# Pruning's first row block loaded into the third product's place, with the row blocks taken in another order

## What is computed

```python
att = softmax(Q @ (H.T @ V).T * scale * H, axis=1);  att_scores = att.mean(axis=0)
comp_mask = softmax(0.5 * structural + 0.5 * att_scores) >= th_comp
xn = x_comp / norm(x_comp);  cos = xn @ xn.T
edge_mask = (softmax(cos * H, axis=1) >= th_edge) & comp_mask[:, None]
H_pruned = H * edge_mask
agg = (H_pruned.T * dv_isqrt[None, :]) @ transformed * (1 / H_pruned.sum(axis=0))[:, None]
msg = dv_isqrt[:, None] * (H_pruned @ agg) @ Theta
```

## Time and profile before

| what | us |
|---|---|
| median of 3 runs | 2440.88 |
| lowest, highest | 2438.64, 2444.03 |
| the profiled execution, its own time | 2440.41 |
| its span in the trace | 2438.5 |
| VectorE busy | 1757.7 (72% of the span) |
| TensorE busy | 2055.7 (84%) |
| ScalarE busy | 779.8 (32%) |
| first to last pruning instruction (L1249), both iterations | 712.0 to 1954.2 |

### The profile page before, as it was taken

One profiled execution on the slowest core, in us unless ns is written; L12 is line 12 of the kernel. 1 busy time (PEld: TensorE's weight loads), 2 busy tenths in 40 slices (PEclk: granted clock), 3 DMA queues, 4 the chain that ended last, 5 costly groups with the idle time before them and its releaser, 6 DMA issues. The chain is left out here.

```text
span 2438.5 us, 36215 instructions
## 1 busy us (share of the span) xinstructions
PE 2055.7 (84%) x15608; PEld 732.7 (30%) x15608; DVE 1757.7 (72%) x2037; ACT 779.8 (32%) x990; POOL 4.5 (0%) x18
## 2 busy tenths in 40 slices
PE   6798959989977766699999989987676689996897
PEld 2224324323221111143344323221111134334333
DVE  7875982268879999965541348879999975553998
ACT  0001000146644333311111036653333311111897
POOL 0000000000000000000000000000000000000000
PEclk9999989999988888899999999988888899997999
DMA  9975989989939999987779989929999987763796
GB/s 385 421 336 233 427 356 425 427 328 376 373 132 424 420 411 410 370 317 277 276 278 386 427 326 376 379 106 411 412 411 410 375 330 270 269 252 156 311 421 253
DMA packets 123486, 834.18 MB, mean 342 GB/s; under 512 B 8512, under 2 KB 10560, under 8 KB 76608
## 3 DMA queue, kind: packets, MB, share of 16 engines
q1 hardware_dynamic: 121136, 829.48, 85.0%
q10 hardware_dynamic: 2192, 2.40, 0.3%
HBM read 695.54 MB, written 136.31 MB: 341 GB/s over the span
## 5 line engine op out<-in xcount | busy, mean ns | idle before, releaser
L923 ACT ACTIVATE stream<-stream,negmax 128x4096 f32<-128x4096 f32 x128 | 475.2, 3713 | 521.4 <-DVE negmax L917 521.4
L912 DVE CUSTOM_DVE_ANT_0 stream<-ps,stream 128x1024 f32<-128x1024 f32 x352 | 413.9, 1220 | 55.3 <-PE ps L876 31.9
L876 PE MATMUL ps<-edgeT,node_twice 64*128 64x512 f32 x1024 | 281.0, 669 | 183.5 <-DVE mx L912 183.4
L455 PE MATMUL ps<-stream,stage 128*64 128x512 f32 x1728 | 387.8, 600 | 42.8 <-DMA stream<-in_adjT 27.4
L876 PE MATMUL ps<-edgeT,query_twice 64*128 64x512 f32 x1024 | 249.6, 619 | 6.3 <-DVE edgeT L944 4.0
L1209 PE MATMUL ps<-stream,xw 32*64 32x512 f32 x4096 | 230.5, 595 | 3.7 <-issue 3.0
L455 PEld LDWEIGHTS ps<-stream,stage 128*64 128x64 f32 x1728 | 122.1, 138 | 300.6 <-issue 221.5
L876 PEld LDWEIGHTS ps<-edgeT,node_twice 64*128 64x128 f32 x1024 | 94.2, 201 | 377.9 <-DVE mx L912 267.6
L894 PE MATMUL ps<-stream,ones 128*1 128x512 f32 x1024 | 185.4, 862 | 11.1 <-DVE stream L1249 11.1
L1249 DVE SCALAR_TENSOR_TENSOR stream<-stream,cut 128x4096 f32<-128x4096 f32 x40 | 179.4, 4484 | 1.4
L1427 DVE SCALAR_TENSOR_TENSOR query_twice<-stream,query_twice 128x512 bf16<-128x512 f32 x256 | 154.7, 679 | 4.6 <-ACT query_twice L1405 4.5
(11 more groups left out here) (195 smaller groups left out, 1692.9 us busy)
## 6 DMA issues: line engine op xcount, KB each, us to landing
stream<-in_adj SPq DMA_DIRECT2D x136, 2048.0 KB, 13.0
stream<-in_adjT SPq DMA_DIRECT2D x74, 2048.0 KB, 13.2
pruned<-stream SPq DMA_DIRECT2D x64, 2048.0 KB, 10.5
spare<-in_adj SPq DMA_DIRECT2D x26, 2048.0 KB, 10.3
spare<-pruned SPq DMA_DIRECT2D x22, 2048.0 KB, 11.5
query_twice<-pruned SPq DMA_DIRECT2D x22, 2048.0 KB, 11.3
node_twice<-pruned SPq DMA_DIRECT2D x20, 2048.0 KB, 11.5
query_twice<-in_adj SPq DMA_DIRECT2D x14, 2048.0 KB, 15.7
```

The costliest lines, as they stand in the source:

```text
L455: last = nc.tensor.matmul(ps[F * h:F * h + F, bank + b, :], stage[:, t.k % SL, :], half_bank(src, b, h), start=False, stop=False, skip_gro ...
L876: last = nc.tensor.matmul(ps[:, 2 * slot + h, :], stationary[F * h:F * h + F, rows_n], bank_of(edgeT[F * h:F * h + F, :], c), start=True, ...
L912: nc.vector.tensor_tensor_reduce(out=prod[s][:, cols], in0=ps[:, 2 * slot:2 * slot + 2, :].rearrange("p a b -> p (a b)"), in1=block_in[:, ...
L923: nc.scalar.activation(prod[s], prod[s], ACT.Exp, bias=negmax[:, s:s + 1], accum_out=zsum[:, s:s + 1]).then_inc(exp_done, 1)
```

## The change

Pruning gets a sixth place for a row block, used once: `prod[2]`, the third product, which is first written in step 2. Step 0 takes its row block from there. The order of the blocks and of the places is changed to fit. Steps 1 to 4 take the four blocks left by `attend`, step 5 uses q2. Block 26 is loaded into `prod[2]`, block 27 into q2 right behind it, both at the beginning of the phase. Step 0 frees no place for a load, so that SP issues none after the store of step 0. VectorE waits in step 2 until step 0 is pruned. q2 is last used in step 30 instead of step 29, and chunk 1 is issued a step later.

```diff
-                seq = [*range(22, NB), *range(22)]
-                R, LEAD = 4, 11
+                seq = [26, 22, 23, 25, 24, *range(27, NB), *range(22)]
+                R, LEAD = 5, 11
+                places = [held[0], held[1], held[3], held[2], held[4]]
+                first_loaded = sem("first_block_loaded")
...
                 def buffer(t):
-                    return held[t.k % HELD]
+                    return prod[2] if t.n == 0 else places[(t.n - 1) % HELD]
...
                     def load(n):
-                        sp.dma_start(held[n % HELD], adj_b[seq[n]]).then_inc(loaded[n % HELD], 16)
-
+                        sp.dma_start(places[(n - 1) % HELD], adj_b[seq[n]]).then_inc(loaded[(n - 1) % HELD], 16)
+
+                    sp.dma_start(prod[2], adj_b[seq[0]]).then_inc(first_loaded, 16)
                     load(R)
                     for n in range(NB):
                         sp.wait_ge(pruned, n + 1)
                         sp.dma_start(Hp[seq[n]], prod[n % SL3]).then_inc(stored[n % SL3], 16)
-                        if n + HELD < NB:
+                        if n >= 1 and n + HELD < NB:
                             load(n + HELD)
                         if n == 28:
                             wait_stored(10)
                             load_chunk(0)
-                        if n == 29:
+                        if n == 30:
                             wait_stored(18)
                             load_chunk(1)
...
                     def body(t):
                         s = t.k % SL3
-                        if t.k >= R:
-                            dve.wait_ge(loaded[t.k % HELD], 16 * (t.turn(HELD, R) + 1))
+                        if t.n == 0:
+                            dve.wait_ge(first_loaded, 16)
+                        if t.n == 2:
+                            dve.wait_ge(pruned, 1)
+                        if t.n >= R:
+                            dve.wait_ge(loaded[(t.n - 1) % HELD], 16 * ((t.n - 1) // HELD + (1 if (t.n - 1) % HELD == HELD - 1 else 0)))
```

## The result

| | before | after |
|---|---|---|
| median (22 runs each) | 2440.31 us | 2447.31 us |
| lowest, highest | 2434.49, 2449.19 | 2441.57, 2453.29 |
| ratio to before, 95% interval | | 1.0029, 1.0020 to 1.0039 |
| span of the profiled execution | 2438.5 | 2449.8 |

The change makes the kernel slower by 7.0 us (4.9 to 9.5 by the interval), where 3.2 us were forecast. The direction and the range held, the forecast size was less than half of what came. 7.0 us lies above the 4.9 us that the prediction called the limit of what can be told, and the lower end of the interval lies on it. By that limit what the prediction gave 0.22 came true, and what it gave 0.66 did not.

A forecast was written before the change was run, and what follows sets the result against it. Pruning was taken to be bound by its DMA traffic. A loss of 5.2 us at the end less a gain of 2.0 at the front made +3.2 us, so 2444.1 us from 2440.9, with an 8-in-10 range of 2438.4 to 2448.5 us.

The forecast's parts named there:

- what the prediction gave 0.22: Whole kernel: the chance that the change measures slower, beyond the 0.2% (4.9 us) that can be told.
- what it gave 0.66: Whole kernel: the chance that the time stays within 0.2% (4.9 us), counted as no change.
- What bounds the stage: Middle of pruning: DMA traffic sets the pace, 10.1 us a step against VectorE's 9.3; VectorE waits for stores.
- Rival A: Pruning: the whole load is saved, 10 us over two passes, giving 2431 to 2436 us; chance 0.09.
- The front: Start of pruning: the store of step 1 lands sooner; net gain 0.5 us in pass 1, 1.5 in pass 2.
- the wait: Step 2 of pruning: VectorE's new wait for the instruction just issued costs 0.26 us, off the gain.
- The end: End of pruning: chunk 1 after step 30 leaves the queue empty; later chunks come late, 3.0 + 2.2 = 5.2 us lost.
- B: Pruning: VectorE's waits are for free row-block places; a sixth removes 36 us, to about 2405 us; chance 0.02.
- C: Start of pruning: two loads share the DMA engines, first block late, 6.4 us more, 2450.5 us; chance 0.06.
- D: End of pruning: chunks 2 and 3 land when they did, only the front's gain remains, 2438.9 us; chance 0.08.
- The chances: Whole kernel: own forecast 0.75; with the rivals, faster 0.12, within 0.2% 0.66, slower 0.22.

The follow-up runs named there:

- without load 15: Kernel before without the load for step 15, mid-pruning, in each pass (output differs): 2435.60 us beside 2439.06, ratio 0.9986.
- without load 5: Kernel before without the load for step 5, the first behind a store, in each pass (output differs): 2437.85 us beside 2439.06, ratio 0.9995.
- chunk 1 back: Changed kernel with places reordered so that chunk 1 is issued after the store of step 29 again: 2438.93 us beside 2439.06, ratio 1.0001.
- order only: Kernel before with only the order of blocks and places changed as in the changed kernel: 2440.64 us beside 2439.94, ratio 1.0003.
- only chunk 1 late: Kernel before with only chunk 1 moved, issued after the store of step 30 instead of 29: 2445.17 us beside 2439.06, ratio 1.0027.
- early chunks: New front as in the changed kernel, chunks 0 and 1 issued one step earlier than in the kernel before: 2444.84 us beside 2439.92, ratio 1.0023.

## Why the prediction was right or wrong

**What bounds the stage: right as far as it went.** Pruning goes at the pace of its traffic, and VectorE waits for stores. But the text spoke of the queue as if it might be deep. It took "5.0 us less traffic" to be true wherever the queue does not run empty; without load 15 a load less in the fullest part gave 1.7 us a pass, and the queue did run empty behind the hole (share 0.12). So the stage has its traffic as its pace as long as nothing is taken out, but VectorE's own pace is not far behind (9.3 us of work in a step of 10.1), and a load is worth less than its bytes even in the middle. Rival A falls by more than the prediction had against it.

**The front, 2.0 us of gain: right up to S1, wrong behind it in pass 1.** S1 lands as forecast in both passes (7.2 us after its issue instead of 8.0 and 9.0), and the wait costs 0.21 us. But "all later transfers queue behind it one by one, so the gain stays what it is there" does not hold in pass 1: S2 lands 27.2 us after S0's issue in both traces. Part of that is S2's issue, 0.3 us later after the change. But without load 5 and without the new wait the lead melts too: 0.8 us at S1, 0.4 at S2, 0.1 at S4. In this part of pass 1 the stores are issued at VectorE's own pace, 9.4 to 9.5 us apart, less than the 10.1 us of a full queue, and no step waits for a store before step 6. In pass 2, where S1 had taken 9.0 us before, the gain did stay, 2.0 us in the mean. What makes the two passes differ was not tested. Over both passes the traces show 1.1 us, and the run with chunk 1 back, which has this front and the old end, is at 1.0001 (-2.4 to +2.9 us).

**The end, 5.2 us of loss: the right step, mis-sized.** This is the term that failed. From the last pruning to the turning of chunk 6:

| | pass 1, us | pass 2, us |
|---|---|---|
| chunk 1 at step 29 (before twice, order only, chunk 1 back, no load 5, no load 15) | 46.1, 46.0, 45.5, 45.4, 45.4, 47.9 | 46.3, 46.0, 47.5, 47.1, 46.6, 47.3 |
| chunk 1 at step 30 (changed twice, only chunk 1 late) | 50.4, 50.1, 50.2 | 49.2, 49.4, 49.1 |
| difference of the means | 4.2 | 2.5 |

So 6.7 us in place of 5.2, near the upper bound of 7. As much is in the landing of C2: over the same traces it lands 3.9 us (pass 1) and 2.8 us (pass 2) later after the last pruning, where 3.0 and 2.2 were forecast. Two pieces of the difference are seen in the first trace of the changed kernel. S30 took 7.6 and 7.7 us to land, not the 7.2 taken from S0. And S31, now behind a chunk instead of behind a store, landed 5.4 us after its forerunner, where it was 5.0 and 4.9 before the change. That makes some 1.8 us in both passes.

A third piece could be suspected. The 16 KB packets of another queue, which the page lists as `instruction`, hold one of the 16 DMA engines for about 1.1 us each, and the transfer in flight then lands 0.7 to 1 us later than its spacing; this was seen in the order of events, not tested. In pass 1 of before such a packet falls 9.5 us after the last pruning, on C2. In the three traces with chunk 1 late the first comes at 28.5, 23.1 and 9.7 us, on C4, C3 and S31, and the stretch is 50.4, 50.1 and 50.2 us all the same. So these packets don't explain what pass 1 costs more than pass 2. Why it does stays open.

**Sum.** 6.7 - 1.1 = 5.6 us from the stretches, 7.0 us (4.9 to 9.5) from the runs, 3.2 forecast. Of the 3.8 us that are missing, the end has 1.5 and the front 0.9; the other 1.4 are within the scatter.

**The rivals.** B: VectorE's waits did not go (35.8 us against 36.3). The rule that it was taken from (Trainium skill, Perfetto Trace Analysis, "Optimization Strategy") may still hold if the missing buffer is a fourth product; no run here shows it. C: the first load landed after 8.0 us with another behind it. D: chunk 1 late alone costs 6.6 us, so the end is not covered. The rule of a fixed 2 us for each transfer (Trainium skill, SBUF — State Buffer, "The DMA setup-cost knee") has the sign of what the front and the end did. Its fit gives 6.8 us at this size; the runs have 6.3 us for a store with nothing near it and 7.2 to 7.7 for one with another transfer close behind.

**The chances.** A sum of 3.2 us with a limit of 4.9 left 1.7 us of room above, and the stated bounds of the end alone reached 1.8 above its value. "Slower" deserved more than 0.22. The end's bounds were 0 to 7 where it was priced and 3 to 7 in the chances, with what lies below left to rival D.

## What to carry to other kernels

In this stage, a transfer taken out was worth about what the transfer behind it gained, or less, and that has to be read at that place: when the issuing engine had nothing to put in its stead, the queue ran empty and most of the gain was lost. Follow the lead further than the next transfer, too: in pass 1 it was gone one step later. Before counting a load as its bytes over the rate, ask what limits the depth of the queue; here, by the code, the wait for a store three steps back. And follow a change of places to the end of the stage: the last use of a place decides when the next stage's first load can start, and one chunk a step later cost over three times what the earlier load could bring.

## What the runs showed of the hardware

A store that finds the queue empty lands sooner still when nothing follows it closely. S0 has L5 0.4 us behind it before the change and took 7.2 us; after the change nothing follows it for 10 us:

```profile
pruned<-stream SPq DMA_DIRECT2D x1, 2048.0 KB, 6.3
```

The kernel without load 5 has the same 6.3 us for S0 in pass 1, with nothing else changed. So the transfer behind does take about 1 us from the one in front. S1, with a load right behind it, landed in the 7.2 us that were forecast.

TensorE's granted clock fell after short waits for DMA. In the kernel with early chunks, after 3.00 us without work it was granted 0.50, the lower of its two levels (1.2 GHz), for the next 3.5 us, and 16 matmuls took 6.60 us instead of 3.65. In all traces here the gathers of chunks 2 and 3 behind a wait of 3.00 us or more were slow (eight, 5.23 to 6.60 us). Below that the length of the wait alone does not decide. After the 2.42 us shown above the gather took 3.65 us; without load 15 a wait of 2.44 us was followed by 5.20 us, and in the second trace of before one of 2.55 us by 3.65:

```profile
1042.99 5.20 PE L1181 MATMUL ps<-spare,moved 128*64 128x512 f32 x16 [2.44 <-DMA spare<-pruned]
...
1042.99:1045.50 2.51, 2.51 (x6) 0.82 (x8) 2.51 (x1) 0.00 (x0) 0.00 (x0) 0.50 1.04 385
...
1048.08 3.65 PE L1181 MATMUL ps<-spare,moved 128*64 128x512 f32 x16 [2.55 <-DMA spare<-pruned]
```

In the changed kernel the wait of 4.90 us for chunk 2 did the same (windows of the wait and of the gather behind it):

```profile
1040.00:1044.20 4.20, 0.00 (x1) 0.03 (x1) 1.40 (x2) 0.00 (x0) 0.00 (x0) 0.97 1.05 388
1044.20:1047.80 3.60, 3.60 (x10) 1.26 (x12) 3.60 (x1) 0.00 (x0) 0.00 (x0) 0.56 1.05 387
```

There it cost nothing by luck: the slowed gather ended at 1049.43, and chunk 3 landed at about 1049.5. A wait for a transfer can thus cost more than its length. The Trainium skill (Perfetto Trace Analysis, "Matmul Optimizations") says that the engine scales with its use, so that matmuls should come back to back; these rows agree that a gap can cost speed, and show that a gap of 2.4 to 2.6 us may or may not.
